# Linear attention with a routed feed-forward layer: keys and values as three products of high and low terms

## The reference, cut to what matters

```python
q = (layernorm(x) @ Wq + bq)            # 16 heads
k = (ctx @ Wk + bk);  v = (ctx @ Wv + bv)
qp = elu(q) + 1;  kp = elu(k) + 1
out_t = qp_t @ sum_{s <= t} kp_s (outer) v_s   # per head
Z = cumsum(qp, axis=tokens)
x = x + (out / Z) @ Wo + bo
h = relu(layernorm(x) @ W1 + b1)
sel = argmax(softmax(h @ W2 + b2))
x = x + layernorm(x) @ expert_W[sel] + expert_b[sel]
```

## Time and profile before

| what | value |
|---|---|
| median of three runs | 1085.85 us |
| the profiled execution's own time | 1082.15 us |
| its span | 1080.4 us |
| TensorE busy in the span | 1011.4 us, 94% |
| VectorE busy | 884.8 us, 82% |
| GpSimd busy | 669.2 us, 62% |
| ScalarE busy | 374.7 us, 35% |
| TensorE's mean granted clock | 0.981 of full speed |
| TensorE's share of the chain that ended last | 81% |

### The profile page before, as it was taken

The page is one execution under the profiler, slowest core; times in us unless marked ns, Lnnn a source line. Parts: engine busy times, 40 slices in busy tenths (PEclk is TensorE's granted clock), DMA queues, the critical chain, the costliest instruction groups (busy, mean ns, idle before and its releaser), DMA issues.

```text
span 1080.4 us, 37750 instructions
## 1 busy us (share of the span) xinstructions
PE 1011.4 (94%) x15784; PEld 721.9 (67%) x15784; DVE 884.8 (82%) x1924; ACT 374.7 (35%) x581; POOL 669.2 (62%) x576
## 2 busy tenths in 40 slices
PE   5689999999999999999999999999999999998873
PEld 2356666676677777766777777667777776676653
DVE  5579888888898888889888888898879888998552
ACT  1333333344333333333333333433333334332210
POOL 4334555557666666676666666766666667655665
PEclk9889999999999999999999999999999999999887
DMA  5556444445555444554555445545544545441461
GB/s 180 134 163 217 120 113 105 119 133 168 127 160 163 133 116 153 159 168 126 161 163 138 128 139 156 168 127 161 163 135 115 156 155 149 109 130 41 139 215 42
DMA packets 90921, 152.52 MB, mean 141 GB/s; under 512 B 19326, under 2 KB 57857, under 8 KB 90625
## 3 DMA queue, kind: packets, MB, share of 16 engines
q1 hardware_dynamic: 67184, 107.03, 36.7%
q0 software_dynamic: 12672, 33.84, 8.6%
q10 hardware_dynamic: 10896, 9.25, 2.8%
HBM read 98.20 MB, written 36.13 MB: 124 GB/s over the span
## 4 chain that ended last, share of the span: by engine, by line
PE 81%; DVE 6%; DMA 4%; issue 4%; POOL 3%; ACT 1%; SPq 0%; DVEq 0%; POOLq 0%
PE b_a L1030 26%; PE b_b L1035 18%; PE b_s L1132 9%; PE b_s L1057 6%; PE b_b L1080 5%; PE b_b L1090 5%; PE b_s L1070 3%; PE b_a L1025 3%; PE b_s L1098 2%; PE b_s L1117 2%; PE b_b L1132 2%; DVE stage L734 1%; DMA scales<-rstd 1%; DMA scale<-scales 1%; DMA buckets<-row,place 1%
## 5 line engine op out<-in xcount | busy, mean ns | idle before, releaser
L734 DVE TENSOR_TENSOR stage<-b_s,causal 128x1024 f32<-128x1024 f32 x192 | 225.7, 1217 | 11.7 <-PE b_s L1070 6.7
L517 POOL DMA_INDIRECT out<-rows x116 | 140.6, 1212 | 36.5 <-issue 31.0
L510 POOL DMA_INDIRECT buckets<-row,place x128 | 141.3, 1104 | 34.3 <-issue 33.7
L1030 PE MATMUL b_a<-x_T,wq_sb 128*128 128x512 f32 x256 | 129.2, 629 | 12.6 <-POOL x_T L537 7.2
L1030 PE MATMUL b_a<-ctxT,wk_sb 128*128 128x512 f32 x256 | 121.4, 618 | 11.0 <-DMA bias_k<-in_L_xattn_bk 9.6
L1035 PE MATMUL b_b<-wo_sb,attT 128*128 128x256 f32 x512 | 120.1, 388 | 6.2 <-DVE attT L948 6.2
L526 POOL TENSOR_TENSOR onehots<-onehots,onehot 128x32 bf16<-128x32 bf16 x32 | 7.8, 244 | 186.3 <-DVE place L875 186.3
L1035 PE MATMUL b_b<-wv_sb,ctxT 128*128 128x256 f32 x512 | 118.9, 385 | 0.0
L553 POOL TENSOR_TENSOR x_res<-x_res,bias_o 128x1024 f32<-128x1024 f32 x32 | 106.1, 3315 | 20.6 <-DMA x_res<-in_x 20.3
L1132 PE MATMUL b_s<-we_sb,x3T 128*128 x464 | 112.4, 385 | 2.9 <-DVE rows L841 2.2
L602 ACT ACTIVATE ex<-b_a,bias_k 128x512 f32<-128x512 f32 x64 | 44.0, 687 | 201.0 <-PE b_a L1030 186.8
(11 more groups left out here) (134 smaller groups left out, 1816.0 us busy)
## 6 DMA issues: line engine op xcount, KB each, us to landing
x_in<-in_x SPq DMA_DIRECT2D x32, 512.0 KB, 4.3
ctxT<-in_ctx SPq DMA_DIRECT2D x32, 512.0 KB
x_T<-in_xT SPq DMA_DIRECT2D x32, 512.0 KB, 4.7
qsel<-qp SPq DMA_DIRECT2D x256, 64.0 KB, 2.4
x_res<-in_x SPq DMA_DIRECT2D x32, 512.0 KB
rows<-buckets SPq DMA_DIRECT2D x116, 130.0 KB
scale<-scales ACTq DMA_DIRECT2D x32, 256.0 KB, 4.8
stage<-buckets SPq DMA_DIRECT2D x20, 130.0 KB, 3.5
```

Of the source, the lines that this page charges most:

```text
L510: pool.indirect_dma_start(buckets, bass.IndirectOffsetOnAxis(place[:, slot(route), t:t + 1], 0), row[:, slot(route), t, :], None).then_inc ...
L517: pool.indirect_dma_start(out.rearrange("t p n -> (t p) n"), bass.IndirectOffsetOnAxis(rows_of(i)[:, TOKEN:TOKEN + 1].bitcast(U32), 0), ro ...
L734: dve.tensor_tensor(dst.rearrange("p g h s q -> p g (h s) q"), b_s[:, :, 256 * t:256 * t + 256].rearrange("p g (a q) -> p g a q", q=C), ca ...
L1030: last = pe.matmul(dst, w[:, k, P * h:P * h + P], rows[:, k, :], start=(k == 0), stop=(k == KC - 1))
```

## The change

The change makes each factor of the key and value products in two parts. A part called high is a copy of a float32 tile into a tile of type float32r, and a part called low is the tile less its high part, also float32r. A product is then high by high, high by low and low by high, each as one float32r matmul. It does this for groups 2 to 31; groups 0 and 1 keep plain float32 products.

- The weights' parts are made once (two copies on ACT in step 2, two subtractions on DVE).
- The context's parts are made each step: `ctx_high` is a copy on ACT (128x1024) after the second half of the queries, `ctx_low` a subtraction on POOL (128x1024) as the last work of POOL's step. TensorE's keys wait for the low part.
- Keys become 12 matmuls of 512 columns, values 24 matmuls of 256 columns.
- POOL scatters two tiles of output, then multiplies z, then scatters the other two; two tiles of bucket rows stand ahead of the reciprocal roots and two behind them.
- DVE makes the values first and then both halves of the keys' feature map, all behind the second pair of masks.
- `x_in`, `x_res` and `ctxT` have one buffer instead of two; SP's waits change with them.

```diff
-        wk_sb = sb("wk_sb", [P, KC, D])
-        wv_sb = sb("wv_sb", [P, KC, D])
+        wk_parts = [sb(f"wk_{part}", [P, KC, D], F32R) for part in ("high", "low")]
+        wv_parts = [sb(f"wv_{part}", [P, KC, D], F32R) for part in ("high", "low")]
-        ctxT = sb("ctxT", [P, 2, KC, N])
+        ctxT = sb("ctxT", [P, KC, N])
+        ctx_parts = [sb(f"ctx_{part}", [P, KC, N], F32R) for part in ("high", "low")]
...
@@ SP: context and residual, one buffer each @@
                 if norm and group_no(norm) >= AHEAD:
-                    sp.wait_ge(s_v, n(norm, 2, -2))
+                    if group_no(norm) == AHEAD:
+                        sp.wait_ge(s_v, 2)
+                    else:
+                        sp.wait_ge(s_clow, n(norm, k=-AHEAD))
                     load_context(norm)
                 if attend:
-                    if group_no(attend) >= 2:
-                        added = held(sp, n(attend, 2, -2))
-                        sp.wait_ge(s_const, POOL_MADE)
-                        sp.wait_ge(s_x1, added)
+                    if group_no(attend) >= 1:
+                        sp.wait_ge(s_x1, n(attend, 2))
...
@@ POOL's step @@
                 if attend:
+                    scatter(slots_of(j - 1)[0:2])
                     pool.wait_ge(s_zinv, n(attend, k=1))
                     pool.tensor_tensor(z[:, :], z[:, :], u[:, :], ALU.mult).then_inc(s_zprod, 1)
-                    scatter(slots_of(j - 1))
+                    scatter(slots_of(j - 1)[2:4])
...
                 if route and j < STEPS - 2:
-                    scatter_rows(route)
+                    scatter_rows(route, range(2))
                 if attend:
                     scatter(extra_slots_of(j))
...
+                if route and j < STEPS - 2:
+                    scatter_rows(route, range(2, GT))
+                if norm and group_no(norm) >= AHEAD:
+                    pool.wait_ge(s_chigh, n(norm, k=1 - AHEAD))
+                    pool.tensor_tensor(ctx_parts[1][:, :, :], ctxT[:, :, :], ctx_parts[0][:, :, :], ALU.subtract)\
+                        .then_inc(s_clow, 1)
...
@@ ACT's step, behind first_queries(norm, 1) @@
+                if norm and group_no(norm) >= AHEAD:
+                    act.wait_ge(s_ctx[slot(norm)], 16 * half(norm) + 16)
+                    act.wait_ge(s_v, n(norm, 2))
+                    act.activation(ctx_parts[0][:, :, :], ctxT[:, :, :], ACT.Copy).then_inc(s_chigh, 1)
...
@@ DVE's step @@
-                if in_place(project):
-                    keys(project, 0)
                 if attend:
                     dve.wait_ge(s_sb, n(attend, k=1))
                     for t in range(2):
                         masked(sc1[:, 2 + t, :, :, :, :], t, t, s_mb)
                 if in_place(project):
+                    values(project)
+                    keys(project, 0)
                     keys(project, 1)
-                    values(project)
...
@@ PE @@
+            def pairs_of_parts(weights, rows):
+
+                for k in range(KC):
+                    for a, b in ((0, 0), (0, 1), (1, 0)):
+                        yield weights[a][:, k, :], rows[b][:, k, :], k == 0 and a + b == 0, k == KC - 1 and a == 1
+
+            def channels_first_parts(dst, weights, rows, h):
+                for w, r, start, stop in pairs_of_parts(weights, rows):
+                    last = pe.matmul(dst, w[:, P * h:P * h + P], r, start=start, stop=stop)
+                return last
+
+            def tokens_first_parts(dst, rows, weights, t):
+                for w, r, start, stop in pairs_of_parts(weights, rows):
+                    last = pe.matmul(dst, r[:, P * t:P * t + P], w, start=start, stop=stop)
+                return last
...
             def keys(group, h):
-                a = slot(group)
                 if h == 0:
-                    pe.wait_ge(s_ctx[a], 16 * half(group) + 16)
-                channels_first(b_a[:, h, :], wk_sb, ctxT[:, a, :, :], h).then_inc(s_k, 1)
+                    pe.wait_ge(s_wlow, 2)
+                    pe.wait_ge(s_clow, n(group, k=1 - AHEAD))
+                channels_first_parts(b_a[:, h, :], wk_parts, ctx_parts, h).then_inc(s_k, 1)
```

More of the change, by code:

```diff
@@ L5 @@
 F32 = mybir.dt.float32
+F32R = mybir.dt.float32r
 BF16 = mybir.dt.bfloat16
@@ L105, in build @@
         we_sb = sb("we_sb", [P, KC, E, D])
[L107 to L109 removed]
+        x_in = sb("x_in", [P, GT, D])
+        x_res = sb("x_res", [P, GT, D])
+        ctxT = sb("ctxT", [P, KC, N])
+        ctx_parts = [sb(f"ctx_{part}", [P, KC, N], F32R) for part in ("high", "low")]
         st1 = sb("st1", [P, GT, 6])
@@ L189, in build @@
         s_xs = sem("s_xs")
+        s_whigh = sem("s_whigh")
+        s_wlow = sem("s_wlow")
+        s_chigh = sem("s_chigh")
+        s_clow = sem("s_clow")
         s_q = sem("s_q")
@@ L341, in ahead, with context_of, x_in_of @@
             return norm if norm and group_no(norm) < AHEAD else None
+        def context_of(t):
+            return ctxT_second if group_no(t) == 1 else ctxT
+        def x_in_of(t):
+            return x_in_second if group_no(t) == 1 else x_in
         def of_x(t):
@@ L636, in step @@
                         keys(norm, h, n(norm, 2, h - 1) if group_no(norm) else 0)
+                    if group_no(norm) == AHEAD - 1:
+                        act.activation(wk_parts[0][:, :, :], wk_sb, ACT.Copy).then_inc(s_whigh, 1)
+                        act.wait_ge(s_wv, VALUE_WEIGHTS)
+                        act.activation(wv_parts[0][:, :, :], wv_sb, ACT.Copy).then_inc(s_whigh, 1)
                 if in_place(project):
@@ L722, in centre_router, with low_weights @@
                                   ALU.subtract).then_inc(s_wcent, 1)
+            def low_weights():
+                for at, (parts, w) in enumerate(((wk_parts, wk_sb), (wv_parts, wv_sb))):
+                    dve.wait_ge(s_whigh, at + 1)
+                    dve.tensor_tensor(parts[1][:, :, :], w, parts[0][:, :, :], ALU.subtract).then_inc(s_wlow, 1)
             def of_mask(which):
@@ L925, in step @@
                                            ALU.mult, ALU.add).then_inc(s_z, 1)
+                if ahead(norm) and group_no(norm) == AHEAD - 1:
+                    low_weights()
                 if 5 <= j < 5 + E // 2:
@@ L1190, in step @@
                         pe.wait_ge(s_qe, n(norm, 4))
-                    keys(norm, 0)
-                    keys(norm, 1)
+                    first_keys(norm, 0)
+                    first_keys(norm, 1)
                     if group_no(norm) == 0:
@@ L1199, in step @@
                         pe.wait_ge(s_vs, n(norm, 2))
-                    values(norm)
+                    first_values(norm)
                     if group_no(norm) == 1:
```

34 lines of the change are left out of this document (23 added, 11 removed).

## The result

The changed kernel takes 1152.76 us, the median of six runs (1148.58 to 1157.44); the kernel before, beside it, 1083.35 (1080.28 to 1088.55). The ratio is 1.063, with a 95% interval of 1.060 to 1.067: slower by 69 us, where 1073 us and a gain were forecast, and outside the range of 1040 to 1106.

The account below looks back on a forecast made before the run. TensorE was taken to bound the kernel, with GpSimd's loop next. Terms -9.7 - 8.9 + 1 + 5 = -12.6 us gave 1069.5 on the profiled execution, 1073 us on the median; 8-in-10 range 1040 to 1106.

Parts of the forecast that it names:

- Rival 3: TensorE's float32r products take two cycles a column: +3.4 us in 30 steps, 1195 us; chance 0.06.
- rival 4: TensorE's loads stand ahead of their matmuls, not hidden: +1.9 us in 30 steps, about 1149 us; chance 0.05.
- The loop through GpSimd: GpSimd's subtraction delays VectorE's picks and what queues behind, TensorE waiting for the rows' sums: a loop of 30.3 us.
- I count zero between -0.05 and +1.3 us a step: VectorE's reordered values and keys: same instructions, later keys' map covered, so zero cost counted within those bounds.
- TensorE's saving: Float32r keys and values at one cycle a column: 0.86 + 0.77 = 1.62 us a step, in 30 steps.
- the early steps: Steps 4 to 9, before expert rows are scattered: the subtraction fits before the picks, whole gain, 6 x 1.62 = 9.7 us.
- the 24 steps (10 to 33): Steps that scatter expert rows: GpSimd's loop leaves a gain of 0.37 us each in place of 1.62, 8.9 in all.
- So the addition should miss it and take 2.38: GpSimd's residual addition misses VectorE's earlier scan and takes 2.38 us, not 3.63; GpSimd's chain becomes 23.3 us.
- The tail: Step 34: two bucket scatters stand behind four extra output scatters; +5 us, between +2.6 and +10.
- Rival 2: Slower: z, residual addition and subtraction all collide with VectorE; loop 31.55 us, 0.88 longer, 1103 us; chance 0.25.
- two inputs: In the waits seen, VectorE has two inputs in SBUF while GpSimd runs a long two-input operation; the later waits.

Follow-up runs that it names:

- the best version: Changed kernel with GpSimd's earlier order, VectorE's second half of the queries' map ahead of the expert rows' sums, full subtraction waiting for that half: 1042.94 us, ratio 0.963.
- e3: Changed kernel with GpSimd's and VectorE's orders of the kernel before; float32r products and full subtraction kept: 1102.02 us, ratio 1.014.
- e2: Changed kernel with VectorE's table of expert rows filled behind the attention's result instead of ahead of it: 1134.61 us, ratio 1.044.
- e1: Changed kernel with the context's subtraction cut to 4 columns of each half instead of 512, from the second group in place on: 1083.59 us, ratio 0.998.
- e11: Changed kernel with GpSimd's order of the kernel before and the subtraction cut to 4 columns of each half: 1058.81 us, ratio 0.976.

## Why the prediction was wrong

- **TensorE: right in kind, a fifth too good.** A float32r instruction takes about 1.1 cycles a column at 2.4 GHz, where one was taken: in the changed kernel a key instruction of 512 columns starts every 0.234 us (0.2145 taken) and a value instruction of 256 every 0.119 (0.1105):

```profile
585.15 0.40 PE L1086 MATMUL b_a<-ctx_high,wk_low 128*128 128x512 f32 x1
585.38 0.40 PE L1086 MATMUL b_a<-ctx_high,wk_high 128*128 128x512 f32 x1
...
589.50 0.28 PE L1091 MATMUL b_b<-wv_high,ctx_high 128*128 128x256 f32 x1
589.62 0.28 PE L1091 MATMUL b_b<-wv_high,ctx_low 128*128 128x256 f32 x1
```

  In the best version keys take 2.99 us with their switch (3.64 before) and values 3.03 (3.65): 1.27 us a step, not 1.62. 30 steps of it are 38 us; that version gained 40. Rival 3 fell, and rival 4 with it: loads of 0.19 us on record hide in a pitch of 0.119, on the same rows of the array, so the rule of the Trainium skill that stood beside this rival ("TensorE: Matmul & The Clock Gate", "What overlaps and what doesn't") does not hold for these instructions. Rival 4's 1149 us are near the result by chance.
- **The loop through GpSimd: right in odd steps alone.** Forecast 30.3 us, measured 30.2, with `tied` held 3.07 us and TensorE idle ahead of the sums.
- **The step that failed: "I count zero between -0.05 and +1.3 us a step"**, the price of VectorE's new order and of z's new place. The map's first half waited from 593.16 for the rest of a scatter and then for the whole of z: 4.20 us for the pair. The prediction saw that z might slip in; it took the old 1.97 us as the price, though that wait began when z was nearly half done. Its rule that the later operation waits for the earlier one missed the scatter, which the earlier trace rows already showed: that `u` began at 994.77, ahead of the residual addition (995.02) but inside a scatter (994.03 to 995.00), and still waited for the whole of the addition. With z alone back in its place (e10) the same kernel takes 1076.90 us, 76 less and 4 over the forecast. That it comes so near is partly luck, since TensorE's saving and the early steps were forecast too good.
- **Where the lost reserve was paid: "the 24 steps (10 to 33)" were taken as alike**, from one odd step of the trace. Every other one fills a table of 13 small operations ahead of the attention's result, in the very place that the moved subtraction reaches once VectorE is late. The prediction names no table and no price for the idle clock; TensorE's wait there and its slow product are some 6 of the 7 us that the even step shown lost.
- **"So the addition should miss it and take 2.38": it did** (mean 2424 ns), but the prediction asked only what the collision does to GpSimd. `u` paid for it, 2.85 us for 1.21. Together the two made VectorE 3.2 us longer in a step than before (4.20 - 2.62 and 2.85 - 1.21); it had 1.09 + 1.23 us idle in an even step and 3.14 + 1.24 in an odd one.
- **The early steps gained nothing like 1.62 each.** Steps 5 to 7 take 83.9 us, as before (the best version 80.0), and step 8, the first with a table, 33.9 for 29.7. The tail lost 3.3 us in step 34 where 5 was counted.
- **Rival 2 was the right kind**, a collision everywhere, and sized for the old orders: its loop is what e3 then ran at. It had no clock in it and no VectorE.

## What to carry to other kernels

Where two engines shut each other out, price a moved operation on both sides: not only what it waits for, but who stands in its way and what is queued behind that one, in each kind of step that the kernel has. Let the long operation of the one run where the other reads PSUM, and wait for that place explicitly: the fastest version here holds its subtraction back for 3 us. And an engine with idle time in sum may have none in the place that a new operation reaches.

## What the runs showed of the hardware beyond that

- The size of VectorE's operation does not matter: one of 1x8 waited 3.02 us. Some with a single SBUF input waited as well, which the prediction's "two inputs" left out: in e2 `whole` for 2.85 us and, in ten other even steps, `taken_sum` for 3.0. Not all do: the statistics of `x_in` (128x256) took 0.42 us at most beside a long GpSimd operation, in all fourteen traces.
- VectorE waited through two GpSimd operations on end, a scatter under way and the long one behind it (593.16 to 596.19, and 610.14 to 613.13); it did not get in between. A scatter does not hold it from its start: beside that of 609.80 two small operations, at 609.87 and 610.06, took 0.15 and 0.16 us.
- After 3.37 us of idle time TensorE's granted clock stood at 0.50 for most of a product. Shorter idle times had both outcomes: in the odd step shown, 0.90 and 0.99 us lie in windows at 1.00, but two steps later 0.90 and 1.05 us were followed by 3.3 us at 0.50, in which a key instruction starts every 0.43 us in place of 0.234:

```profile
650.28 0.19 PE L1205 MATMUL b_a<-onehot,before 128*128 128x32 bf16 x1 [0.90 <-DVE onehot L1013]
651.90 1.17 PE L1123 MATMUL b_s<-qsel,kp 32*128 32x128 f32 x32 [1.05 <-DVE rows L880]
653.40:656.70 3.30, 3.30 (x9) 2.56 (x8) 3.26 (x8) 1.02 (x2) 2.58 (x2) 0.50 0.62 93
```
- In e1 TensorE stops in the middle of the late sums in 24 steps, for up to 1.7 us and 24.4 us in all, with nothing named by the profile; the kernel before has next to nothing of it (0.8 us there), e11 9.2 us, the best version 2.4. What it waits for was not tried and stays open. It may be part of why e11 lies 16 us over the best version: between steps 14 and 32 e11 is 0.33 us a step slower, all of it in the sums over the values.
